# Vision-transformer layer: the inner activations turned by transposing DMAs, the feed-forward's loads and stores issued by sync

## The reference

```python
h = bitlinear(x, w_in, g_in)            # x = layernorm(h), 192 -> 2 * 512
up, gate = jnp.split(h, 2, axis=-1)
y = jax.nn.silu(gate) * up              # 512 inner activations a row
return bitlinear(y, w_out, g_out)       # 512 -> 192, added to the residual
```

## Time and profile before

| | us |
|---|---|
| median of 3 runs | 1250.26 (1249.92 to 1251.47) |
| the profiled execution, whole | 1249.54 |
| its span | 1247.5 |

### The profile page before, as it was taken

One profiled execution on the slowest core, in us unless ns is written; L12 is line 12 of the kernel. 1 busy time (PEld: TensorE's weight loads), 2 busy tenths in 40 slices (PEclk: granted clock), 3 DMA queues, 4 the chain that ended last, 5 costly groups with the idle time before them and its releaser, 6 DMA issues.

```text
span 1247.5 us, 32691 instructions
## 1 busy us (share of the span) xinstructions
PE 1113.8 (89%) x11182; PEld 676.2 (54%) x11182; DVE 1062.5 (85%) x1979; ACT 929.0 (74%) x1877; POOL 461.3 (37%) x540
## 2 busy tenths in 40 slices
PE   7999996699999999999999999999478777777878
PEld 6999995145555555555555555555344444444444
DVE  6666778179999999999999999999879888888885
ACT  0000000599999999999999999999279889899986
POOL 5544444002111332221112211112267666666663
PEclk9999998599999999999999999999679999999998
DMA  8999995145556556655555565555423333323322
GB/s 290 329 281 291 289 318 181 45 132 145 144 145 144 150 152 159 158 145 147 146 144 144 146 153 155 155 152 137 114 55 96 85 93 88 93 83 95 88 83 68
DMA packets 158364, 187.70 MB, mean 150 GB/s; under 512 B 42865, under 2 KB 119745, under 8 KB 158017
## 3 DMA queue, kind: packets, MB, share of 16 engines
q1 hardware_dynamic: 90656, 138.99, 35.0%
q10 hardware_dynamic: 52224, 37.37, 9.8%
q0 software_dynamic: 15360, 9.70, 8.2%
HBM read 143.06 MB, written 36.12 MB: 144 GB/s over the span
## 4 chain that ended last, share of the span: by engine, by line
PE 61%; ACT 17%; issue 9%; ACTq 5%; DVE 4%; DMA 3%; SPq 1%; POOL 0%; DVEq 0%; POOLq 0%
PE psum L1155 12%; PE psum L1218 12%; PE psum L1090 10%; PE psum L1188 7%; PE psum L1158 7%; PE psum L1171 6%; PE psum L1205 5%; ACT yi L620 5%; ACT ysq L640 3%; ACT big L613 3%; ACT zi L628 3%; ACTq L659 2%; ACTq L656 2%; ACT big L604 1%; DMA big<-w_tok 1%
## 5 line engine op out<-in xcount | busy, mean ns | idle before, releaser
L724 POOL DMA_DIRECT2D h_res<-att x128 | 135.1, 1178 | 557.5 <-ACT att L558 548.3
L1035 DVE TENSOR_TENSOR pi<-big 128x2364 int16<-128x2364 f32 (+1 forms) x128 | 333.3, 2604 | 8.1 <-DMA big<-z_row 6.7
L582 ACT ACTIVATE big<-psum 128x788 f32<-128x788 f32 (+1 forms) x384 | 330.4, 862 | 0.2 <-DVE pi L1035 0.2
L544 ACT ACTIVATE qki<-psum 128x394 int16<-128x394 f32 x384 | 172.5, 509 | 17.5 <-PE psum L1158 5.6
L1090 PE MATMUL psum<-big 128*128 128x192 f32 (+1 forms) x1128 | 182.4, 326 | 0.0
L1090 PEld LDWEIGHTS psum<-big 128*128 128x128 f32 (+1 forms) x1128 | 180.6, 188 | 1.1 <-DVE big L826 0.3
L1218 PE MATMUL psum<-big,sa_hot 128*32 128x197 f32 (+1 forms) x3072 | 168.9, 337 | 0.6 <-DVE zt L1059 0.6
L544 ACT ACT_TABLE_LOAD x1 | 1.3, 1283 | 224.3 <-PE psum L1158 224.3
L757 POOL TENSOR_TENSOR big<-big,goutb 128x512 f32<-128x512 f32 (+1 forms) x99 | 124.0, 1273 | 63.7 <-DVE big L1002 63.7
L1155 PE MATMUL psum<-xT,w1b 128*128 128x394 bf16 x384 | 108.5, 342 | 25.0 <-DMA xT<-x_int 16.1
L1205 PE MATMUL psum<-qkb 64*128 64x197 bf16 (+1 forms) x1536 | 129.9, 247 | 0.0
(11 more groups left out here) (107 smaller groups left out, 1805.2 us busy)
## 6 DMA issues: line engine op xcount, KB each, us to landing
big<-z_row SPq DMA_DIRECT2D x192, 394.0 KB, 5.0
big<-xt SPq DMA_DIRECT2D x98, 384.0 KB, 4.5
tin<-h_res SPq DMA_DIRECT2D x49, 192.0 KB, 2.4
tres<-h_res ACTq DMA_DIRECT2D x49, 192.0 KB, 2.5
out<-oo ACTq DMA_DIRECT2D x49, 192.0 KB, 2.6
h_res<-big ACTq DMA_DIRECT2D x78, 96.0 KB, 4.4
h_res<-att POOLq DMA_DIRECT2D x64, 96.0 KB, 3.1
x_int<-big ACTq DMA_DIRECT2D x93, 64.0 KB, 4.1
```

The source lines that it names most:

```text
L544: act.activation(qki[:, k, :, :], psum[:, bank, 0:2 * N] .rearrange("p (c n) -> p c n", c=2), ACT.Copy, scale=factor[(F_Q, F_K)[b % 2]])\
L582: act.activation(ex[0:r, tri, t, 4 * g:4 * g + 4, :].rearrange("p (a h) n -> p a h n", a=2), psum[0:r, 2 * t:2 * t + 2, 0:2 * N] .rearrang ...
L724: pool.dma_start(h_res[bass.ds(b - 4, 1), t0:t0 + r, :].rearrange("a n d -> (a n) d"), att[0:r, par, t, :], accum_op=ALU.add).then_inc(s_a ...
L1035: v.tensor_tensor(pi[0:r, t, :, 0:N], ex[0:r, it, t, :, :], zb[0:r, ip, :, :], ALU.mult).then_inc(s_pi, 1)
```

## The change

The eight transposes of yi on PE and ACT's copy of their result are gone. In their place SP issues one transposing DMA a pair, right after yi is ready: it reads yi3 (128 rows x 1024 int16) and writes the integers turned into `yTi`, which lies in the space of attention's `qki`. DVE converts them to bf16 with one copy into `yT3`, two steps later (pair t - 6), between L985 and L944. The second linear layer, the output and the store each come one step later than before (pairs t - 6, t - 6 and t - 7), and the pipeline has one step more. The loads of `tres` and the stores of the output move from ACT's queue to SP's, ahead of the load of tin in SP's order. The scale 1 / 512 and the epsilon of y's mean square go elsewhere: g_out is multiplied by sqrt(512) once, at the start, and y gets a 513th column with the constant sqrt(512e-6), so that the sum of the squares holds the epsilon already; POOL's L735 goes. The squares are taken over 513 columns, and `yy` has a new place.

```diff
         s_t = {k: sem("ffn_" + k) for k in (
             "stats", "mean_var", "zc", "amax", "vareps", "x_rms", "step", "factors", "dequant", "xi",
-            "xT_summed", "xT_read", "hid", "silu", "y", "square", "yg", "y_amax", "yms", "y_rms",
-            "yi", "yT_summed", "yT_read", "o_summed", "o_ready")}
+            "xT_summed", "xT_read", "hid", "silu", "y", "square", "yg", "y_amax", "y_rms",
+            "yi", "yT_read", "o_summed", "o_ready")}
         s_t3 = [sem(f"ffn_in_{p}") for p in range(2)]
         s_t3b = [sem(f"ffn_residual_{p}") for p in range(2)]
+        s_ym = [sem(f"ffn_y_turned_{p}") for p in range(2)]
...
-        CONST_STEPS = 24
+        CONST_STEPS = 25
...
-        LAGS = 7
+        LAGS = 8
...
+        yTi = qki[:, :, :, :].rearrange("p a b n -> p (a b n)")[:, 0:2048].rearrange("p (i k n) -> p i k n", i=2, k=8)
...
-        silu, yy = [xflat[:, 2 * k * HID:2 * (k + 1) * HID].rearrange("p (a b) -> p a b", a=2) for k in (2, 3)]
-        ysq = sb("ysq", [128, HID], bf16)
+        silu = xflat[:, 4 * HID:6 * HID].rearrange("p (a b) -> p a b", a=2)
+        yy = big[:, o_pt + n_pt:o_pt + n_pt + 2 * (HID + 1)].rearrange("p (a b) -> p a b", a=2)
+        ysq = sb("ysq", [128, HID + 1], bf16)
...
+                if pair(5) or pair(7):
+                    wait_apart(sp, s_t["o_ready"], min(t - 6, NPAIR) if isinstance(t, int) else t - 6)
+                if at := pair(5):
+                    r, n = at
+                    sp.dma_start(tres[0:r, oth, 0:n, :], pair_rows(h_att, t - 5, r, n)).then_inc(s_t3b[oth], 16)
+                if at := pair(7):
+                    r, n = at
+                    sp.dma_start(pair_rows(out, t - 7, r, n), oo[0:r, oth, 0:n, :]).then_inc(s_t3o[oth], 16)
                 if at := pair(-1):
                     r, n = at
                     if isinstance(t, int):
                         wait_added(sp, t + 1)
                     wait_apart(sp, s_t["zc"], t)
                     sp.dma_start(tin[0:r, oth, 0:n, :], pair_rows(h_att, t + 1, r, n)).then_inc(s_t3[oth], 16)
+                if at := pair(4):
+                    r, n = at
+                    wait_apart(sp, s_t["yi"], t - 3)
+                    wait_apart(sp, s_t["yT_read"], t - 5)
+                    sp.dma_start_transpose(yTi[:, par, 0:4 * n, 0:r], yi3[0:r, par, 0:n, :].rearrange("p a h -> p (a h)"))\
+                      .then_inc(s_ym[par], 16)
 
...
-                if at := pair(5):
-                    r, n = at
-                    act.wait_ge(s_t["yT_summed"], t - 4)
-                    act.activation(yT3[:, 0:n, :, 0:r], psum[:, 5, :].bitcast(i16)
-                                   .rearrange("p (a c n) -> p a c n", a=2, c=4)[:, 0:n, :, 0:r], ACT.Copy)\
-                       .then_inc(s_t["yT_read"], 1)
...
-                    wait(act, s_t["yT_summed"], t - 5)
+                    if not isinstance(t, int) or t > 5:
+                        act.wait_ge(s_ym[par], loads_of(t - 6, par))
...
-                            wait(act, s_t["yms"], t - 4)
+                            wait(act, s_t["y_rms"], t - 4)
...
-                if pair(4) or pair(6):
-
-                    wait(act, s_t["o_ready"], min(t - 5, NPAIR) if isinstance(t, int) else t - 5)
-                if at := pair(4):
-                    r, n = at
-                    if isinstance(t, int):
-                        wait_added(act, t - 4)
-                    act.dma_start(tres[0:r, par, 0:n, :], pair_rows(h_att, t - 4, r, n)).then_inc(s_t3b[par], 16)
-                if at := pair(6):
-                    r, n = at
-                    act.dma_start(pair_rows(out, t - 6, r, n), oo[0:r, par, 0:n, :]).then_inc(s_t3o[par], 16)
...
-                    g.tensor_scalar(val(1, par, MS, r, n), val(1, par, T_, r, n), 1.0 / HID, RMS_EPS,
-                                    ALU.mult, ALU.add).then_inc(s_t["yms"], 1)
-                    pool.wait_ge(s_t["yms"], t - 3)
-                    g.tensor_tensor(val(1, par, RMS, r, n), val(1, par, MS, r, n), neg_half[0:r, 0:n], ALU.pow)\
+                    g.tensor_tensor(val(1, par, RMS, r, n), val(1, par, T_, r, n), neg_half[0:r, 0:n], ALU.pow)\
                         .then_inc(s_t["y_rms"], 1)
...
-                        g.tensor_tensor(yg[0:r, oth, a, :], yy[0:r, a, :], goutb[0:r, :], ALU.mult)\
+                        g.tensor_tensor(yg[0:r, oth, a, :], yy[0:r, a, 0:HID], goutb[0:r, :], ALU.mult)\
                             .then_inc(s_t["yg"], 1)
...
+            const(v.tensor_scalar(goutb[:, :], goutb[:, :], float(HID) ** 0.5, None, ALU.mult))
...
+            v.memset(yy[:, :, HID:HID + 1], (HID * RMS_EPS) ** 0.5).then_inc(s_wdeq4, 1)
+            dve.wait_ge(s_wdeq4, 3)
...
+                if at := pair(6):
+                    r, n = at
+                    dve.wait_ge(s_ym[par], loads_of(t - 6, par))
+                    wait(dve, s_t["o_summed"], t - 6)
+                    v.tensor_copy(yT3[:, 0:n, :, 0:r], yTi[:, par, 0:4 * n, 0:r]
+                                  .rearrange("p (a c) n -> p a c n", c=4)).then_inc(s_t["yT_read"], 1)
...
-                        v.scalar_tensor_tensor(yy[0:rr, a, :], psum[0:rr, 2 * a, :], ft[0:rr, (q + 2) % 4, 0, a:a + 1],
+                        v.scalar_tensor_tensor(yy[0:rr, a, 0:HID], psum[0:rr, 2 * a, :], ft[0:rr, (q + 2) % 4, 0, a:a + 1],
                                                silu[0:rr, a, :], ALU.mult, ALU.mult).then_inc(s_t["y"], 1)
-                if at := pair(5):
-                    r, n = at
-                    dve.wait_ge(s_t["o_summed"], t - 4)
-                    dve.wait_ge(s_t["dequant"], t - 1)
-                    dve.wait_ge(s_t3b[oth], loads_of(t - 5, oth))
-                    if not isinstance(t, int) or t > 6:
-                        dve.wait_ge(s_t3o[oth], loads_of(t - 7, oth))
+                if at := pair(6):
+                    r, n = at
+                    dve.wait_ge(s_t["o_summed"], t - 5)
+                    dve.wait_ge(s_t["dequant"], t - 2)
+                    dve.wait_ge(s_t3b[par], loads_of(t - 6, par))
+                    if not isinstance(t, int) or t > 7:
+                        dve.wait_ge(s_t3o[par], loads_of(t - 8, par))
                     for a in range(n):
-                        ins = v.scalar_tensor_tensor(oo[0:r, oth, a, :], psum[0:r, 6, a * D:(a + 1) * D],
-                                                     ft[0:r, (q + 3) % 4, 1, a:a + 1], tres[0:r, oth, a, :],
+                        ins = v.scalar_tensor_tensor(oo[0:r, par, a, :], psum[0:r, 6, a * D:(a + 1) * D],
+                                                     ft[0:r, (q + 2) % 4, 1, a:a + 1], tres[0:r, par, a, :],
                                                      ALU.mult, ALU.add)
                     ins.then_inc(s_t["o_ready"], 1)
...
-                if at := pair(5):
-                    r, n = at
-                    pe.wait_ge(s_t["yi"], t - 4)
-                    wait(pe, s_t["yT_read"], t - 5)
-                    dst = psum[:, 5, :].bitcast(bf16).rearrange("p (a c n) -> p a c n", a=2, c=4)
-                    for a in range(n):
-                        for c in range(4):
-                            last = nc.tensor.transpose(dst[:, a, c, 0:r], yi3[0:r, oth, a, c * 128:(c + 1) * 128].bitcast(bf16),
-                                                       ident[0:r, 0:r])
-                    last.then_inc(s_t["yT_summed"], 1)
...
-                if at := pair(5):
-                    r, n = at
-                    pe.wait_ge(s_t["yT_read"], t - 4)
-                    wait(pe, s_t["o_ready"], t - 5)
+                if at := pair(6):
+                    r, n = at
+                    pe.wait_ge(s_t["yT_read"], t - 5)
+                    wait(pe, s_t["o_ready"], t - 6)
                     for a in range(n):
                         for c in range(4):
                             last = mm(psum[0:r, 6, a * D:(a + 1) * D], yT3[:, a, c, 0:r], woutb[:, c, :],
```

More of the change, by code:

```diff
@@ L925, in _ @@
                 v.tensor_copy(wdeq4[:, k, :], wdeq[:, k:k + 1].to_broadcast([128, 2])).then_inc(s_wdeq4, 1)
-            dve.wait_ge(s_wdeq4, 2)
+            v.memset(yy[:, :, HID:HID + 1], (HID * RMS_EPS) ** 0.5).then_inc(s_wdeq4, 1)
+            dve.wait_ge(s_wdeq4, 3)
             def pair_step(t, par, q):
```

## The result

The changed kernel takes 1228.96 us (median of 4 runs, 1227.86 to 1232.45) against 1250.09 for the kernel before: a ratio of 0.9834, 95% interval 0.9815 to 0.9854, or 21 us less. The forecast was 1239.0, its range 1231 to 1264. The direction was right, and DVE did become the engine that waits for no other, but the gain came out nearly twice as large, and the time lies 2 us under the range.

The account below looks back on a forecast made before the run. ACT's own sum was taken as the bound before, DVE's 6.30 us after: 43 x (6.565 - 6.30) = 11.4 us less, + 0.4 + 0.5 = -10.5 against 1249.54, giving 1239.0 us, range 1231 to 1264.

Parts of the forecast that it names:

- ACT's own sum: ACT's work per feed-forward step, said to set the pace before: 6.45 us, falling to about 5.2 after.
- Most of the 0.42 us gap, say 0.35: ACT's idle time after issuing the output's store; moving the DMA issues was to save 0.35 us a step.
- the cycle of the squares: Loop from ACT's squares through POOL and DVE's factors back to yi: 6.25 us before, 5.97 after, a close limit.
- The long steps around the stores: Stalls of over 1 us on ACT, which its new slack may absorb or which may reappear on SP or DVE.
- DVE's sum: DVE's chain per step, 5.88 us plus 0.42 for the copy: 6.30 us, the new bound.
- The ends: Lower and upper values for DVE's step after the change: 6.22 and 6.42 us.
- T = 2.7: SP's issue of the transposing DMA of yi: 2.7 us a step, hidden under DVE's 6.30.
- the formula: Cycle over tin's load, spanning two steps of length P: 8.84 + T = 2P, giving P = 5.8, hidden.
- The tail: The last, short steps plus one extra pipeline step: +0.5 us, from -1.5 to +3.
- The constant: One scaling of g_out among DVE's constants, done once: 0 to 0.5 us, 0.4 taken.
- PE's clock: Rival: PE's clock falls and stays at 1.2 GHz, giving 1350 us; chance 0.03, against gaps of about 0.5 and 0.8.
- The rule of the page "VectorE: DVE Perf Modes": Each 128x128 square paid for by itself in yi's transposing DMA; rival at 1.21 us a square, 1455 us, chance 0.04.

Follow-up runs that it names:

- M alone: The kernel before with only the mean square's part (scale in g_out, constant column, POOL's L735 gone): 1251.44 us, ratio 1.001.
- Q alone: The kernel before with only the residual loads and output stores moved from ACT's queue to SP's: 1227.88 us, ratio 0.9813.
- M + Q: The kernel before with the mean square's part and the DMAs' move to SP, without the transposing DMA: 1225.82 us, again 1225.00 us.
- the repeat: The changed kernel itself, unaltered, timed again beside the kernel before on one chip: 1230.92 us, ratio 0.983.

## Why the prediction was wrong, step by step

- **ACT's own sum sets the pace before: right.** M alone is worth nothing; Q alone 22 us. "Most of the 0.42 us gap, say 0.35" was a little low: Q alone gives 0.39 in straight code and 0.48 in the loop, with the cycle of the squares as the next limit, and M + Q gives 0.46 (6.34 to 5.88), where ACT runs without a gap. The long steps around the stores, some 3 us in all, were left outside the sum and named in the range only.
- **DVE's sum is the bound after: right in kind, wrong in size, and this is the step that failed.** The prediction put 5.88 + 0.42 = 6.30 us and measured is 6.044; 43 x 0.256 = 11.0 us, more than the whole miss of 10.0. Two thirds of it lie between the start of L985 and L944: 1.22 + 0.42 = 1.64 was put, 1.47 measured. The reduction's 1.22 us counted whole, although the next instruction starts after 1.14, and the copy counted 0.42 where a second copy adds 0.34. The prediction had named this overlap of 0.1 us a line and taken it off the lower end only. The other third, 0.09 a step, is in the stretch from L944 to L985: 4.66 in the one step that was read, 4.47 in straight code after the change and 4.56 to 4.71 in the loop. One step of the loop had been taken for all. And part of what was added up as DVE's own work is a path through POOL: the 3.36 us from L1005 to L982 end with POOL's product in every full step, so "DVE's own sum" is right as a length, but not shown to be the only limit of that length.
- **The ends were too close.** 6.22 and 6.42 were built around 5.88 as if that were exact. Straight-code steps of before, 6.34 less the 0.55 us of idle time ahead of L944, were 5.79; with a copy of 0.34 that is 6.13, already below the lower end.
- **The cycle of the squares: too long.** Where it does set the pace, with Q alone and L735 still in it, the step is 5.95 in straight code and 6.12 in the loop, for the 6.25 put. In straight code 0.2 us of the difference lie ahead of L735: it starts 0.09 us after the squares there and 0.29 in the step that was read.
- **The transposing DMA, T = 2.7: wrong, without harm, and by luck.** It took 1.25 us. With two issues, 2.7 us together, the average step is 6.22: under the 6.30 that the prediction compared with, but over the 6.04 that was measured. The price was over twice too high, and the formula, which gave 5.8, let too much pass; the two errors offset each other.
- **The tail: inside its range** (+0.5 taken, +0.06 measured, -1.5 in the repeat), as a cost of 1.4 to 3.0 us for the transposing DMA's extra step against a gain of 3.0 from the other two parts (25.4 to 22.5). The constant: 0.7 us for 0.4.
- **PE's clock: right,** 1.00 in the window, gaps of 0.74 to 0.80 ahead of L1272. The rival was live: with the copy moved to the end of the factors PE waited up to 2.1 us and the granted clock was 0.87 to 0.96.
- **The rule of the page "VectorE: DVE Perf Modes"** in the Trainium skill, 1309 ns by DMA for a 128x128 transpose, is not borne out as a price by the square: eight squares take 3.1 us (median) from issue to landing, 0.39 us each.

The direction survived because ACT's relief was sure. Which part bought it, the prediction did not see: it counted 0.91 us for the copy and 0.35 for the issues, but the issues alone are enough, since below them ACT's chain and DVE's (5.88) and the cycle (5.95) lie within 0.1 us of each other.

## What to carry to other kernels

Before pricing a relief, add up every engine's chain from starts to starts, never from durations, over several steps, and look for a second relief that reaches the same floor: here moving two DMA issues off the bounding engine gave all that the change as a whole gives. A busy engine without idle time may still be held by another engine that finishes at the same moment: compare the end of each input with the start of its reader before calling the sum the only bound. Work added to an engine that will be the bound may lie in the latency behind a reduction, and then its place in the order decides between 0.14 and 0.34 us. Keep DVE's 16-bit SBUF copies away in time from POOL's operations.

## What the runs showed of the hardware

- **DVE's copy and POOL disturb each other.** The copy of 1024 int16 takes 417 ns alone and 648 beside POOL's product; POOL's power of 2 columns takes 0.95 us instead of 0.69 with the copy in its middle. The Trainium skill's page "SBUF — State Buffer" ("SBUF: two separate sides") has a port pair that DVE's fast modes and GpSimd lock against each other for a whole instruction, the first to start winning. The copy agrees with that in the main, since it is the one that grows and ends 0.29 us after the product does; the power does not, since it starts 0.5 us ahead of the copy and still is the one that grows.
- **The issue of a transposing DMA did not grow with its elements:** 1.21 us (median) for 208x256 from HBM, 1.25 for 128x1024 from SBUF, 1.21 for the last pair's 64x512.
- **A dependent operation behind a reduction of 1024 elements** starts 1.33 to 1.35 us after it, an independent one 1.14.
- **Two DMA issues at the end of ACT's step cost its chain 0.46 us a step** in straight code (6.34 against 5.88), and SP takes them for nothing.
